# Placing edges in a four-layer graph kernel: one one-hot of classes instead of two, weights stored class by class

## The reference, cut to what matters

```
edge_index = jnp.stack([src, dst])
x = _layernorm(x + L0(x, edge_index))                 # hypergraph conv: segment sums both ways
x = _layernorm(x + L1(x, edge_attr_64, src, dst))     # edge MLP: edge features, x[src], x[dst]
x = _layernorm(x + L2(x, edge_index))                 # sigmoid gate on k[dst] + q[src]
x = _layernorm(x + L3(x, edge_index))                 # degree-normalized neighbour sum
```

## Time and profile before

| | before |
|---|---|
| time, median of 3 runs | 5115.4 us (5107.4 to 5129.0) |
| the profiled execution: its time | 5113.5 us |
| its span in the profile | 5111.9 us |
| busy: PE, DVE, POOL, ACT | 87%, 68%, 52%, 49% of the span |
| share of the chain that ended last: DMA of `feat_slot` puts | 35% |
| share of that chain: POOL line 775 | 10% |

### The profile page before, as it was taken

The page is one execution under the profiler, slowest core; times in us unless marked ns, Lnnn a source line. Parts: engine busy times, 40 slices in busy tenths (PEclk is TensorE's granted clock), DMA queues, the critical chain, the costliest instruction groups (busy, mean ns, idle before and its releaser), DMA issues.

```text
span 5111.9 us, 162653 instructions
## 1 busy us (share of the span) xinstructions
PE 4452.1 (87%) x63712; PEld 4074.4 (80%) x63712; DVE 3457.2 (68%) x5384; ACT 2505.2 (49%) x3929; POOL 2673.2 (52%) x2387
## 2 busy tenths in 40 slices
PE   1777999979999899999999999998768888888587
PEld 0666888869999888888888888887568888888587
DVE  6999888831110277676676767675369999999812
ACT  0443999930000166666666666665346555555400
POOL 0488555556666677666666667667003333333200
PEclk9998999989999999999999999999869999999898
DMA  5931888899999765555555555553135455554396
GB/s 179 378 129 37 292 323 315 326 302 405 379 418 416 280 199 172 167 172 167 171 172 168 172 163 173 163 172 122 66 90 170 156 157 156 159 158 158 102 385 265
DMA packets 548970, 1093.13 MB, mean 214 GB/s; under 512 B 127323, under 2 KB 455857, under 8 KB 541452
## 3 DMA queue, kind: packets, MB, share of 16 engines
q1 hardware_dynamic: 467738, 973.45, 55.1%
q0 software_dynamic: 73696, 111.71, 7.0%
q10 hardware_dynamic: 7056, 0.91, 0.1%
HBM read 781.88 MB, written 307.92 MB: 213 GB/s over the span
## 4 chain that ended last, share of the span: by engine, by line
DMA 37%; DVE 20%; issue 20%; POOL 11%; PE 8%; POOLq 2%; SPq 1%; ACT 0%; DVEq 0%; ACTq 0%; another core or an unknown queue 0%
DMA feat_slot<-SK,sidx_p 35%; POOL feat_slot L775 10%; DVE arena L2102 5%; PE PS L1073 4%; DVE arena L2111 4%; DVE arena L2125 4%; DVE arena L2131 3%; DVE arena L2103 1%; POOLq L752 1%; PE PS L848 1%; POOL SK L753 1%; DMA sidx_p<-SK 1%; POOLq L775 1%; PE PS L1163 1%; SPq L423 0%
## 5 line engine op out<-in xcount | busy, mean ns | idle before, releaser
L775 POOL DMA_INDIRECT feat_slot<-SK,sidx_p x1764 | 2164.8, 1227 | 1078.5 <-DMA feat_slot<-SK,sidx_p 597.7
L1163 PE MATMUL PS<-arena 128*128 128x128 bf16 x14406 | 1451.4, 221 | 44.0 <-DVE arena L2111 43.9
L1167 PE MATMUL PS<-arena 128*128 128x128 bf16 (+2 forms) x14406 | 1409.8, 207 | 0.0
L1163 PEld LDWEIGHTS PS<-arena 128*128 128x128 bf16 x14406 | 988.3, 99 | 50.2 <-issue 45.3
L1167 PEld LDWEIGHTS PS<-arena 128*128 128x128 bf16 x14406 | 953.6, 99 | 0.0
L2131 DVE TENSOR_TENSOR arena<-arena 128x896 f32<-128x896 f32 (+1 forms) x686 | 585.6, 854 | 382.7 <-ACT arena L1526 378.5
L1535 ACT ACTIVATE arena<-arena 128x896 bf16<-128x896 f32 (+1 forms) x686 | 524.8, 765 | 612.6 <-DVE arena L2131 611.3
L709 POOL TENSOR_TENSOR arena<-arena 128x448 bf16<-128x448 f32 x343 | 355.7, 1037 | 873.8 <-ACT arena L1535 873.8
L1187 PE MATMUL PS<-arena 128*128 128x384 bf16 (+1 forms) x4802 | 708.4, 288 | 116.7 <-POOL arena L709 113.5
L1073 PE MATMUL PS<-arena 128*128 128x192 bf16 (+1 forms) x7203 | 615.2, 248 | 103.1 <-DVE arena L1957 61.6
L1073 PEld LDWEIGHTS PS<-arena 128*128 128x128 bf16 x7203 | 606.2, 98 | 110.5 <-DVE arena L1957 61.8
(11 more groups left out here) (240 smaller groups left out, 5463.9 us busy)
## 6 DMA issues: line engine op xcount, KB each, us to landing
arena<-slot_rows SPq DMA_DIRECT2D x1372, 224.0 KB
arena<-cnt_t SPq DMA_DIRECT2D x147, 896.0 KB
arena<-cnt_t SPq DMA_DIRECT2D x147, 672.0 KB
feat_slot<-zero SPq DMA_DIRECT2D x7, 10976.0 KB, 31.4
cnt_t<-arena SPq DMA_DIRECT2D x49, 1568.0 KB
cnt_s<-arena SPq DMA_DIRECT2D x49, 1568.0 KB
arena<-feat_slot SPq DMA_DIRECT2D x343, 224.0 KB
SK<-in_edge_attr_dram POOLq DMA_DIRECT2D x196, 288.0 KB
```

Source lines behind the costliest of these rows:

```text
L775: pool.indirect_dma_start(feat_slot, bass.IndirectOffsetOnAxis(ap=sidx_p[odd][:, n:n + 1].bitcast(u32), axis=0), fwin[h][:, t * D:(t + 1) ...
L1163: last = nc.tensor.matmul(PS[:, to:to + P], selS[c][:, cut], qsplit[:, (b * 3 + s) * H:(b * 3 + s + 1) * H], start=s == 0 and (k != 4 or j ...
L1167: last = nc.tensor.matmul(PS[:, to:to + w_], selT[c][:, cut], dsplit[odd][:, s * w_:(s + 1) * w_] if k == 4 else dsplit5[:, bass.ds(w * (3 ...
```

## The change

The second one-hot `spread` and the four-fold copy `pay4` are gone, with their semaphores and with ACT's `repeat_pay`. `weigh(w)` multiplies `ohx`, the one-hot that `match_classes` made, with a payload of the window, broadcast over the classes. Its result has the layout of `ohx`: payload, class, column (2 x 49 x 36), with the column innermost. `fill_slots` therefore reads, for a column t, 98 elements that lie 36 elements (72 bytes) apart, where it read 104 contiguous ones. The four padded columns per payload are gone, and so is one preparing copy on DVE (line 1815). `match_classes(w)` has one wait more, since `ohx` of window w-2 must not be overwritten before `weigh(w-2)` has read it.

```diff
-        pay4 = [carve(66 + i, 3 * WT * 4, bf16) for i in range(2)]
-        spread = carve(61.5, WT * NB4, bf16)
-        wpay = [carve(a, WT * 2 * NB4, bf16) for a in (54, 126.5)]
+        wpay = [carve(a, WT * 2 * NB, bf16) for a in (54, 126.5)]
...
-                        last = nc.tensor.matmul(PS[:, 3072:3072 + 2 * NB4], ohr[odd][:, t * P:(t + 1) * P],
-                                                wpay[odd][:, t * 2 * NB4:(t + 1) * 2 * NB4], start=t == 0, stop=t == WT - 1)
+                        last = nc.tensor.matmul(PS[:, 3072:3072 + 2 * NB], ohr[odd][:, t * P:(t + 1) * P],
+                                                wpay[odd].rearrange("p (n t) -> p n t", t=WT)[:, :, t], start=t == 0, stop=t == WT - 1)
...
-                def repeat_pay(w, odd):
-                    if later(w, 0, 2):
-                        act.wait_ge(pay_made, w - 1)
-                    nc.scalar.activation(pay4[odd].rearrange("p (k t a) -> p k t a", k=3, a=4),
-                                         pay[:, :, bass.ds(w * WT, WT)].rearrange("p k (t a) -> p k t a", a=1)
-                                         .to_broadcast((P, 3, WT, 4)), ACT.Copy).then_inc(pay4_made, 1)
...
-                step(V.tensor_copy(pay[:, 0, :], t_f))
...
                     if later(w, 0, 2):
                         dve.wait_ge(before_made, w - 1)
                         dve.wait_ge(prod_made, w - 1)
+                        dve.wait_ge(pay_made, w - 1)
...
-                def spread_classes(w, odd):
...
-                    TT(spread.rearrange("p (t b a) -> p t b a", t=WT, a=4),
-                       pay4[odd][:, 0:4 * WT].rearrange("p (t b a) -> p t b a", t=WT, b=1).to_broadcast((P, WT, NB4 // 4, 4)),
-                       iota1[:, 0:NB4].rearrange("p (t b a) -> p t b a", t=1, a=4).to_broadcast((P, WT, NB4 // 4, 4)),
-                       ALU.is_equal).then_inc(spread_made, 1)
...
                     for k in range(2):
-                        last = TT(wpay[odd].rearrange("p (t k b a) -> p t k b a", t=WT, k=2, a=4)[:, :, k, :, :],
-                                  spread.rearrange("p (t b a) -> p t b a", t=WT, a=4),
-                                  pay4[odd][:, (k + 1) * 4 * WT:(k + 2) * 4 * WT].rearrange("p (t b a) -> p t b a", t=WT, b=1)
-                                  .to_broadcast((P, WT, NB4 // 4, 4)), ALU.mult)
+                        last = TT(wpay[odd].rearrange("p (k b t) -> p k b t", k=2, b=NB)[:, k, :, :],
+                                  ohx[odd].rearrange("p (b t) -> p b t", b=NB),
+                                  pay[:, k + 1, bass.ds(w * WT, WT)].rearrange("p (b t) -> p b t", b=1).to_broadcast((P, NB, WT)),
+                                  ALU.mult)
...
-                        spread_classes(w - 1, (w - 1) % 2)
```

More of the change, by code:

```diff
@@ L47 @@
 BANK_BLOCKS = ((0, 1), (2, 3), (4, 5), (6,))
-NB4 = -(-NB // 4) * 4
 RB = 3
@@ L293, in build @@
         pay_made = sem("pay_made")
-        pay4_made = sem("pay4_made")
-        spread_made = sem("spread_made")
         ohr_made = sem("ohr_made")
@@ L1353, in keep_slots @@
                         act.wait_ge(rows_made, w)
-                    o = PS[:, 3072:3072 + 2 * NB4].rearrange("p (k b) -> p k b", k=2)[:, :, 0:NB]
+                    o = PS[:, 3072:3072 + 2 * NB].rearrange("p (k b) -> p k b", k=2)
                     nc.scalar.activation(sd1[:, 0:2 * NB].rearrange("p (k b) -> p k b", k=2), o, ACT.Copy)
@@ L1366, in body @@
                         keep_totals(w, odd)
-                        repeat_pay(w, odd)
                     if not isinstance(w, int) or w >= 3:
@@ L1842, in match_slots @@
                         .then_inc(ohr_made, 1)
-                def spread_classes(w, odd):
-                    dve.wait_ge(pay4_made, w + 1)
-                    if later(w, 0, 1):
-                        dve.wait_ge(pay_made, w)
-                    TT(spread.rearrange("p (t b a) -> p t b a", t=WT, a=4),
-                       pay4[odd][:, 0:4 * WT].rearrange("p (t b a) -> p t b a", t=WT, b=1).to_broadcast((P, WT, NB4 // 4, 4)),
-                       iota1[:, 0:NB4].rearrange("p (t b a) -> p t b a", t=1, a=4).to_broadcast((P, WT, NB4 // 4, 4)),
-                       ALU.is_equal).then_inc(spread_made, 1)
                 def weigh(w, odd):
@@ L1857, in weigh @@
                         dve.wait_ge(slots_made, w - 1)
-                    dve.wait_ge(spread_made, w + 1)
                     for k in range(2):
-                        last = TT(wpay[odd].rearrange("p (t k b a) -> p t k b a", t=WT, k=2, a=4)[:, :, k, :, :],
-                                  spread.rearrange("p (t b a) -> p t b a", t=WT, a=4),
-                                  pay4[odd][:, (k + 1) * 4 * WT:(k + 2) * 4 * WT].rearrange("p (t b a) -> p t b a", t=WT, b=1)
-                                  .to_broadcast((P, WT, NB4 // 4, 4)), ALU.mult)
+                        last = TT(wpay[odd].rearrange("p (k b t) -> p k b t", k=2, b=NB)[:, k, :, :],
+                                  ohx[odd].rearrange("p (b t) -> p b t", b=NB),
+                                  pay[:, k + 1, bass.ds(w * WT, WT)].rearrange("p (b t) -> p b t", b=1).to_broadcast((P, NB, WT)),
+                                  ALU.mult)
                     last.then_inc(pay_made, 1)
```

## The result

The changed kernel takes 5291.7 us (median of 4 runs, 5285.8 to 5314.7) against 5111.4 us before (median of 4; one run more than in the table above). The ratio is 1.036, with a 95% interval of 1.032 to 1.041. The range on record ended at 5135: the forecast was wrong, and what came is the side of rival 3, larger than I had priced it. The profiled execution took 5314.7 us, 201 us more than that of before.

What follows compares the result with a forecast made beforehand. The puts were taken to bound the kernel's end, DVE to pace placing. Placing's 48 us saved less 34 handed back gave -14 from 5113.5, 5099.5, or 5102 us as median; range 5072 to 5135.

Steps and rivals of the forecast that it cites:

- rival 3: PE in placing: a strided column costs four times as much, 172 ns a matmul; +67 us, 5182 us; chance 0.13.
- the low end: PE's strided read in placing: the contiguous rate holds, 98 columns in 43 ns, 0.1 us less per window.
- The high bound: PE's strided read in placing: f32 rate of 1.23 ns a column, 120 ns a matmul, +2.7 us a window.
- The rule of the Trainium skill: SBUF has 16-byte lines; a different line for each access costs a penalty, with no size given for PE.
- rival 2: PE in placing: the strided read costs twice as much, 86 ns a matmul; 5112 us; chance 0.27.
- the slack: Path of placing, counts, layer 0 and slot pass was said to have 75 us to spare beside the puts.
- a put needs two seams between DVE instructions: POOL's puts in placing: six DVE instructions a window give three puts, five give 2.5.
- my 22 missing puts: Puts by the end of placing: 81 instead of 103, made up in the slot pass at 34 us.
- the page of the Trainium skill: Prediction said the trace differs from its inference that tensor_tensor does not hold up descriptor generation; puts end at tensor_tensor seams.
- the zeroing of `feat_slot`, which DVE does not set: First put hangs 46.98 us from 191.77 behind this zeroing, so puts start at 239 us as before.
- the 14 us that I gave it: Whole-kernel gain: 48 us saved in placing, 34 handed back as longer waits for puts at line 554.

Runs made afterwards that it cites:

- e6: Changed kernel with fill_slots reading 98 contiguous elements per column (wrong numbers in the slots) and 32 of 36 puts a window: 5044.1 us, ratio 0.9844.
- e5: Kernel before without the puts of every ninth column, 32 of 36 puts a window: 5075.1 us beside 5121.6, ratio 0.9914.
- the contiguous read: Changed kernel with fill_slots reading 98 contiguous elements per column instead of a step of 36 (wrong numbers in the slots): 5058.1 us beside 5117.8, ratio 0.9885.

## Why the prediction was wrong

**The strided read.** This is the step that failed: "I take the low end, since the other operands of the same width (bf16) are all at 0.42 to 0.44 ns a column". Those operands were contiguous, so they bounded nothing about a step; that the width is the same was no ground. What the runs showed in its place: a matmul that reads at a step of 72 bytes takes 186 ns and not 43, 1.9 ns a column. The high bound, the f32 rate of 1.23 ns, wasn't one either. The rule of the Trainium skill that I quoted spoke against the change, and in that it was right; rival 2, which I tied to it, took a factor of two without a row for it. Only rival 3 had about the size (172 ns a matmul), at a chance of 0.13, and its factor of four was no better founded.

**Rival 3's sum.** It gave +67 us, +180 came. Its window was 10.5 us and is 12.4. Of the 1.9 us, 0.5 is the price (14 ns x 36), and most of the rest is the clock: the sum took PE's other work at the 4.1 us of the earlier trace rows, and with a mean of 0.56 granted it took 5.7, although PE was busy for 600 of 612 us. And the slack was 41 us, not 75: that is what the slot pass lost when the waits went. SP's waits are for loads that PE needs only later (the last one ends 57 us before the end of the pass, with 35.8 us for a window), so the first microseconds of a wait stop nobody.

**DVE.** Right: a window of 6.64 us for 6.55 to 6.6 predicted, products at the pace of `match_classes`, placing at 458 us for 455. The added wait costs 0.2 us instead of 0.12: in e6 the weighings end at 404.63 and the next product starts at 404.76, where without the wait it starts 0.09 ahead of that end.

**ACT.** No run takes ACT's copy away alone; DVE's window came out as predicted with the copy at nothing.

**The puts.** Right: they hold the end of the kernel before (e5, 46 us). Wrong: "a put needs two seams between DVE instructions". Read the earlier trace rows with the earlier trace rows again: 301.67 to 303.45 has the seam of 302.53 in it and ends 0.92 us after it; 303.76 to 305.49 ends 0.93 after the seam at 304.56; 305.79 to 308.94 ends 0.92 after that at 308.02. A put waits for one seam and ends some 0.92 us after it; so do 108 of the 110 puts that the kernel before starts between 240 us and the end of placing (0.85 to 0.99). That most ends also lay near a seam came from products 1 us long. With 0.3 us of issue it then misses the next seam where seams are 1 us apart. That gives three puts a window with six seams and also with five, and the contiguous read has 92 from 256 to 458 us, 30.4 windows: 3.0 each. (There the seam with the wait is wider, and some puts catch the one right behind it, such as one from 308.71 us of 0.97 us, so the measured count and not this rule is what counts.) So the removed instruction cost no put, and 15 of my 22 missing puts never were.

The trace does not contradict the page of the Trainium skill as I wrote either. "SBUF — State Buffer", Who interferes with whom, lets tensor_tensor contend with GpSimd's reads of SBUF, and a put reads its row numbers from `sidx_p`, which lies in SBUF. No run separates that read from the making of the descriptors.

**The start of the puts.** Wrong: "the zeroing of `feat_slot`, which DVE does not set". The put hung beside two things, the zeroing and DVE's unbroken products, and I named the one without checking the other. With the hang gone, 24 more puts are done by 256 us. The sum for the contiguous read by the corrected terms: the kernel before had started 112 puts when placing ended, this one some 124 by 458 us. In the 1600 us of the slot pass that can be compared it does 840 against 849, so 3 of the 12 stay. The last put comes 45 us earlier by placing and 3 / 0.6 = 5 us by these, 50 in all; it starts at 3528.6 instead of 3581.6, 53 us earlier, and the median fell by 60. The remaining 7 us are within the spread of the runs (5038.8 to 5069.4).

So the one question that decided the case, what 72 bytes of step cost, could not be answered from the trace of the kernel before, and I had placed 0.87 of the chance on prices of 120 ns or less. And the gain that the DVE side of the change brings was four times the 14 us that I gave it, a good part of it by way of the first put, whose cause is not shown.

## What to carry to other kernels

A read with a step is priced by the 16-byte lines that it passes over, about 1.8 ns each and at most one line an element, on PE's moving operand. At a step of 72 bytes PE's weight loads (1.8 ns an element) and an ACT copy (1.9) paid the same. Choose the layout so that a line holds several of the wanted elements: runs of four bf16 kept DVE at its pace and halved PE's price, which made the same saving of work a gain of 1.2% instead of a loss of 3.6% (half of the gain is placing, half the shorter slot pass). Where an operand's access has no like in the trace, its neighbours give no bound for it, and the range has to say so.

## What was not expected of the hardware

- PE's granted clock fell to 0.56 in the mean over the 612 us of strided reads, with PE busy 600 us of them. With runs of four PE was busy 350 of 364 us and the clock was 1.00; in the kernel before it was 0.91 with 305 of 392 us busy.
- The price of a step of 8 bytes or more doesn't change with the clock: step 12 took 1.04 us for six matmuls beside a contiguous group of 0.46 us, and 1.03 beside one of 0.26.
- Beside DVE products with both inputs in SBUF, POOL's indirect DMAs stand until the next seam between its instructions (108 of 110 puts in the kernel before), and the first one stood 47 us in all three kernels in which DVE had no gap.
- A product whose innermost run is two bf16 elements takes 1.73 us for 1764 elements, with runs of four or 36 it takes 1.03.
